# A Griffin block with two FFNs in split fp32r on one core: the second FFN begins in round 14 instead of round 10, two units a round

## The reference

```
t   = rmsnorm(x) * n1
xb  = causal_conv4(t @ Wx)
r,i = sigmoid(xb @ Wa), sigmoid(xb @ Wi)
a   = exp(-8 softplus(lam) r);  b = sqrt(max(1 - a*a, 1e-12)) * i * xb
h   = scan(h = a*h + b)
h1  = x + (h * gelu(t @ Wy)) @ Wo
u   = rmsnorm(h1) * n2
ffn = (gelu(u @ Wg) * (u @ Wu)) @ Wd          # first FFN, 256 -> 1024 -> 256
x1  = layernorm(x + h1 + ffn)
out = layernorm(x1 + relu(x1 @ W1 + b1) @ W2 + b2)   # second FFN
```

## Time and profile before

| | |
|---|---|
| median of 3 runs | 600.15 us (599.4 to 600.36) |
| the profiled execution | 600.54 us, its span 598.7 us |
| PE busy | 590.6 us (99% of the span), 3529 matmuls |
| DVE busy | 381.5 us (64%) |
| ACT busy | 317.2 us (53%) |
| POOL busy | 187.1 us (31%) |
| DMA | 15.68 MB, mean 26 GB/s |
| granted TensorE clock | 0.999 |

### The profile page before, as it was taken

The page is one execution under the profiler, slowest core; times in us unless marked ns, Lnnn a source line. Parts: engine busy times, 40 slices in busy tenths (PEclk is TensorE's granted clock), DMA queues, the critical chain, the costliest instruction groups (busy, mean ns, idle before and its releaser), DMA issues.

```text
span 598.7 us, 9284 instructions
## 1 busy us (share of the span) xinstructions
PE 590.6 (99%) x3529; PEld 521.7 (87%) x3529; DVE 381.5 (64%) x700; ACT 317.2 (53%) x601; POOL 187.1 (31%) x287
## 2 busy tenths in 40 slices
PE   8999999999999999999999999999999999999996
PEld 7768888899888998889898988889888898889896
DVE  5889877374856567484774846857478474662565
ACT  5988853654438444375443744356444653323454
POOL 3041353117240352313513153140722215240130
PEclk9999999999999999999999999999999999999999
DMA  8530010001001010010100001010000100010011
GB/s 283 166 106 1 1 36 1 2 1 36 1 1 35 2 37 0 1 36 2 35 2 19 18 1 36 1 36 2 1 1 0 37 2 0 2 36 0 1 37 36
DMA packets 13100, 15.68 MB, mean 26 GB/s; under 512 B 616, under 2 KB 12288, under 8 KB 13056
## 3 DMA queue, kind: packets, MB, share of 16 engines
q1 hardware_dynamic: 13056, 15.09, 7.5%
HBM read 10.89 MB, written 4.19 MB: 25 GB/s over the span
## 4 chain that ended last, share of the span: by engine, by line
PE 91%; DVE 5%; ACT 1%; issue 1%; DMA 1%; POOL 1%; SPq 0%; DVEq 0%
PE psum L361 17%; PE psum L363 17%; PE psum L362 17%; PE psum L372 11%; PE psum L374 11%; PE psum L373 11%; PE psum L379 3%; DMA xs<-in_L_attn_x_dram 1%; PE psum L447 1%; PE psum L575 1%; PE psum L577 1%; PE psum L573 1%; DVE row L1285 1%; PE psum L474 1%; PE psum L414 1%
## 5 line engine op out<-in xcount | busy, mean ns | idle before, releaser
L1662 POOL TENSOR_SCALAR gu_hi<-gu_raw 128x512 fp32r<-128x512 f32 x64 | 52.8, 824 | 313.1 <-DVE gu_raw L1308 310.3
L1318 DVE TENSOR_TENSOR hid_lo<-hid_raw,hid_hi 128x512 fp32r<-128x512 f32 x56 | 45.6, 814 | 84.0 <-ACT hid_hi L952 84.0
L948 ACT ACTIVATE hid_raw<-psum,vecs 128x512 f32<-128x512 f32 x56 | 38.5, 687 | 113.8 <-PE psum L363 113.8
L1308 DVE TENSOR_TENSOR gu_raw<-psum,gu_raw 128x512 f32<-128x512 f32 x64 | 44.1, 689 | 68.4 <-PE psum L363 68.1
L372 PE MATMUL psum<-w_d_hi,gu_hi 128*128 128x256 f32 x256 | 72.8, 284 | 0.2 <-DVE gu_lo L1313 0.2
L372 PE MATMUL psum<-w_hi,hid_hi 128*128 128x256 f32 x256 | 71.7, 280 | 0.2 <-DVE hid_lo L1318 0.2
L374 PE MATMUL psum<-w_hi,hid_lo 128*128 128x256 f32 x256 | 71.8, 281 | 0.0
L374 PE MATMUL psum<-w_d_hi,gu_lo 128*128 128x256 f32 x256 | 71.8, 281 | 0.0
L373 PE MATMUL psum<-w_lo,hid_hi 128*128 128x256 f32 x256 | 71.7, 280 | 0.0
L373 PE MATMUL psum<-w_d_lo,gu_hi 128*128 128x256 f32 x256 | 71.7, 280 | 0.0
L939 ACT ACTIVATE gu_raw<-psum 128x512 f32<-128x512 f32 x64 | 38.3, 598 | 48.6 <-PE psum L363 48.0
(11 more groups left out here) (222 smaller groups left out, 1519.3 us busy)
## 6 DMA issues: line engine op xcount, KB each, us to landing
out_dram<-row SPq DMA_DIRECT2D x15, 256.0 KB, 2.2
xs<-in_L_attn_x_dram SPq DMA_DIRECT2D x7, 512.0 KB, 3.5
raw<-in_L_ffn_W_dram SPq DMA_DIRECT2D x2, 1024.0 KB, 7.9
raw_gud<-in_L_attn_Wg_dram SPq DMA_DIRECT2D x1, 1024.0 KB, 7.4
raw_gud<-in_L_attn_Wu_dram SPq DMA_DIRECT2D x1, 1024.0 KB, 9.5
raw_gud<-in_L_attn_Wd_dram SPq DMA_DIRECT2D x1, 1024.0 KB, 12.7
xs<-in_L_attn_x_dram SPq DMA_DIRECT2D x2, 256.0 KB, 2.9
raw_xyai<-in_L_attn_Wx_dram SPq DMA_DIRECT2D x1, 256.0 KB, 2.6
```

The costliest lines, as they stand in the source:

```text
L948: nc.scalar.activation(hid_raw[:, w % SLOTS, :], bank[:, :], ACT.Relu, bias=vec("b1", m)).then_inc(relu_ready, 1)
L1308: nc.vector.tensor_tensor(gu_raw[:, r % SLOTS, :], up_bank(r)[:, :], gu_raw[:, r % SLOTS, :], ALU.mult).then_inc(gu_ready, 1)
L1318: nc.vector.tensor_tensor(hid_lo[:, w % SLOTS, :], hid_raw[:, w % SLOTS, :], hid_hi[:, w % SLOTS, :].bitcast(FP32), ALU.subtract).then_inc ...
L1662: nc.gpsimd.tensor_scalar(gu_hi[:, r % SLOTS, :], gu_raw[:, r % SLOTS, :], 1.0, 0.0, ALU.mult, ALU.add).then_inc(gu_hi_ready, 1)
```

## The change

**The second FFN.** It begins in round 14 (`FROM`). Rounds 14 to 17 have two units each, and from round 18 (`PACED`) it is again 10 units behind the first. Its splits and chunk 0's way to it move: W1's first piece is split in rounds 9 (hi) and 10 (lo), W1's second and W2's first in 10 and 11, W2's second in 13; chunk 0's statistics in round 11, its normalise in 12, `transpose_x1` at the end of 13, and the split of x1T at the start of 14. Chunk 2's `mix_out`, `add_mix`, `square_h1`, `norm_u` and `transpose_u` move one round on, into rounds 14 and 15.

**Banks.** Gate and up use banks 4 and 5 in rounds 9, 11 and 13 too. From round 18 on they alternate between 0 and 1, and `mlp_up(w)` uses bank w % 2. It waits for `gelu_gate` of its round.

**Rounds 0 to 7.** gate(1) stands ahead of up(0), down(r) moves from round r + 1 to r + 2, and mix_decay(1) with mix_input(1) from round 3 to round 4. Behind round 7 chunk 1's transposes alternate with mix_x(2).

**The prologue.** The first norm's root is taken by ScalarE (`Sqrt` with a table of its own, then `Exp`'s) and VectorE's reciprocal instead of GpSimd's power; the gates' first half alternates Wa and Wi by k; `second_x` is cut by k and put around `first_out`; steps of ScalarE and VectorE are reordered; x + h1 of chunk 0 goes from GpSimd to VectorE in round 3 (`first_add_x`), and SP's load of chunk 2 waits for it. W1 loads in two halves, and W2 behind chunk 2.

The core of the diff:

```diff
-LAG_DOWN = 11
+FROM = 14
+        PACED = KH + LAG_UP
+        ASIDE = (1, 3, 5, 9, 11, 13)
+        def second_units(r):
+            if r < FROM:
+                return ()
+            if r < PACED:
+                return (2 * (r - FROM), 2 * (r - FROM) + 1)
+            return (r - LAG_UP,)
         def gate_bank(r):
-            return psum[SECOND] if r in (1, 3, 5) else psum[GATE]
+            if r < PACED:
+                return psum[SECOND] if r in ASIDE else psum[GATE]
+            return psum[r % 2]
         def up_bank(r):
-            return psum[SECOND + 1] if r in (1, 3, 5) else psum[UP]
+            if r < PACED:
+                return psum[SECOND + 1] if r in ASIDE else psum[UP]
+            return psum[1 - r % 2]
+        def mlp_bank(w):
+            return psum[w % 2]
...
 # TensorE
             def mlp_up(w):
-                if r < UNITS:
-                    pe.wait_ge(gu_ready, r + 1)
+                if w < KH:
+                    pe.wait_ge(gu_ready if w % 2 else gelu_ready, FROM + w // 2 + 1)
+                elif r < UNITS:
+                    pe.wait_ge(gelu_ready, r + 1)
...
             def first_period(r):
-                gate_up(r)
-                if 1 <= r < KH - 1:
-                    down(r - 1)
-                if r == 3:
+                if r != 1:
+                    gate(r)
+                if r == 0:
+                    gate(1)
+                if r >= 2:
+                    down(r - 2)
+                if r == 4:
                     split_done("a", "i")
                     mix_decay(1)
                     mix_input(1)
+                up(r)
...
             def round_of(r):
-                if units(r - LAG_UP):
-                    mlp_up(r - LAG_UP)
-                if units(r - LAG_DOWN):
-                    mlp_down(r - LAG_DOWN)
+                if r == FROM:
+                    split_done("1", "2")
+                for w in second_units(r):
+                    mlp_up(w)
+                    if w == 1:
+                        mix_out(n)
+                    if w >= 1:
+                        mlp_down(w - 1)
+                    if w == 2:
+                        transpose_u(n)
-                if m == 1 and 1 <= p <= CHUNKS:
+                if r == KH + 5 or m == 1 and 2 <= p <= CHUNKS:
                     transpose_x1(p - 1)
...
 # ScalarE, at the end of round_of(r)
+                if r == KH + 1:
+                    weight_hi("1", ks=[0])
+                if r == KH + 2:
+                    weight_hi("1", ks=[1])
+                    weight_hi("2", ks=[0])
+                if r == KH + 5:
+                    weight_hi("2", ks=[1])
...
 # VectorE, in round_of(r)
-                if r == KH or m == 1 and f >= 1 and first:
+                if r == KH + 4 or m == 1 and f >= 1 and first:
                     normalise(f, 0, 0, x1_ready)
                     normalise(f, 0, 1, x1_ready)
-                if m == 2 and first:
+                if (r == FROM or m == 2 and f >= 1) and first:
                     split_lo(x1T_lo, x1T_hi, x1T_hi_ready, x1T_lo_ready, f)
...
                     if m == 5:
                         gated(n)
-                        hy_lo(n)
+                        if p >= 2:
+                            hy_lo(n)
...
                 if units(r):
                     gate_lo(r)
...
+                    if r == KH + 5:
+                        hy_lo(n)
...
+                for w in second_units(r):
+                    hidden_lo(w)
+                    if w == 2:
+                        split_lo(uT_lo, uT_hi, uT_hi_ready, uT_lo_ready, n)
+                if r == KH + 2:
+                    weight_lo("1", ks=[0])
+                if r == KH + 3:
+                    statistics(0, 0, 0, s1_ready)
+                    statistics(0, 0, 1, s1_ready)
+                    weight_lo("1", ks=[1])
+                    weight_lo("2", ks=[0])
+                if r == KH + 5:
                     weight_lo("2", ks=[1])
```

More of the change, by code:

```diff
@@ L77, in griffin_mlp_kernel @@
         h1.append(sb("h1_1", [P, TT, D]))
-        with nc.sbuf_tensor("raw_2", [P, WIDTH], FP32) as raw:
-            raw_of["2"] = raw[:, :]
-        rows = [sb(f"row{i}", [P, TT, D]) for i in range(2)]
+        rows = [sb("row0", [P, TT, D])]
+        with nc.sbuf_tensor("raw_1", [P, H], FP32) as raw:
+            raw_1 = [raw[:, :]]
+        rows.append(sb("row1", [P, TT, D]))
         normed = sb("normed", [P, TT, D])
@@ L381, in transposed, with transposed_by_pairs @@
                     last.then_inc(done, 1)
-            def transposed_by_pairs(src, c, ready, done, bank, fillers):
-                for q in range(PAIRS):
-                    pe.wait_ge(ready, 4 * c + 2 * q + 2)
+            def transposed_by_pairs(src, c, ready, done, bank, fillers, qs=range(PAIRS)):
+                for q in qs:
+                    if ready is u_ready:
+                        if c == 0:
+                            pe.wait_ge(first_u_ready, q + 2)
+                            if q == 1:
+                                pe.wait_ge(ready, u_tiles(0))
+                        else:
+                            pe.wait_ge(ready, u_tiles(c - 1) + 2 * q + 2)
+                    else:
+                        pe.wait_ge(ready, 4 * c + 2 * q + 2)
                     for tt in (2 * q, 2 * q + 1):
@@ L435, in first_x, with second_x @@
                         last.then_inc(half_wx_done if h == 0 else wx_done, 1)
[L437 to L442, removed]
+            def second_x(m, k):
+                pe.wait_ge(second_tT_ready[k], 1)
+                if k == 0:
+                    pe.wait_ge(tanh_i_ready, KD)
+                last = raw_step(psum[MIX + m][:, :], "x", m, k, first_tT[1])
+                if k == KD - 1:
+                    last.then_inc(wx_done, 1)
             def half_step(bank, n, k, h, moving):
@@ L742, in _ @@
                 first_y(h)
-            second_x(0)
+            for m in range(KD):
+                second_x(m, 0)
             pe.wait_ge(w_loaded["o"], DMA)
@@ L770, in square_first_x @@
                     last.then_inc(x_squared, 1)
+                    tiles = slice(2 * q, 2 * q + 2)
+                    act.wait_ge(rms_eps_ready, 1)
+                    act.wait_ge(x_squared, q + 1)
+                    nc.scalar.activation(rstd1[:, tiles], ss1[:, tiles], ACT.Sqrt, bias=rms_eps[:, :],
+                                         scale=1.0 / D).then_inc(rms1_ms, 1)
             def square_x(c):
@@ L1489, in lam_stepped @@
                 dve.wait_ge(lam_step, steps)
-            first_norm_t(0)
+            for q in range(PAIRS):
+                first_norm_t(q)
+            dve.wait_ge(vecs_ready, 1)
+            dve.wait_ge(tT_done, 1)
+            for f in range(KD):
+                nc.vector.tensor_scalar(first_tT[0][:, f, half(0)], pair_bank(MIX, 0)[:, f, :], vec("n1", f), None,
+                                        ALU.mult).then_inc(first_tT_ready[0], 1)
             dve.wait_ge(lam_exp, 1)
@@ L1676, in round_of @@
                     return
-                if r == KH:
-                    for q in range(PAIRS):
-                        ln_scale(0, 0, q)
                 if mixing:
```

242 lines of the change are left out of this document (138 added, 104 removed).

## The result

The changed kernel takes 602.14 us (median of 6 runs, 601.99 to 602.37), the kernel before 599.72 us in runs beside it (6 runs, 599.4 to 600.36). The ratio is 1.0040, with a 95% interval of 1.0028 to 1.0052: slower by 2.4 us. The forecast was 600.4 with a range of 598.3 to 602.0; the measured time lies 0.14 us above the range, and 2.4 us is more than the 1.2 us that the prediction could not tell from no change: it is the slower class, which had a chance of 0.18.

The account below looks back on a forecast made before the run. TensorE, busy for 99% of the span, was taken to bound the kernel, so the forecast counted its idle time. The terms -0.3 - 1.1 + 2.1 - 0.4 = +0.3 us on 600.15 gave 600.4, range 598.3 to 602.0.

Parts of the forecast that it names:

- the slower class: The outcome that the change makes the kernel slower, made up of rivals (c) and (d); chance 0.18.
- the sum of +0.3: Whole kernel: gains of 0.3, 1.1 and 0.4 us against a loss of 2.1, so 0.3 us slower.
- the part on rounds 14 to 17: Second FFN, two units a round: splits have 1.4 us or more each; hid_lo(4) costs 0.1 at most.
- round 60: From round 18 mlp_up waits for gelu instead of gate_times_up, which removes idle; gain 0.4 us.
- the prologue's step: Start to gate(8): gate(0) at 35.0 instead of 36.08, only 0.15 through to mix_decay(1), gate(8) gains 0.3 us.
- Rival (a): First rounds: TensorE's early lead gets through, gate(8) gains 1.3 us instead of 0.3, total 599.4; chance 0.15.
- Rounds 8 to 11: From gate(8) to gate(12): TensorE's idle falls from 1.37 to 0.25 us; gain 1.1.
- Rival (c): Rounds 8 to 13: VectorE becomes the bound and gu_lo comes late for down, total 602.2 us; chance 0.13.
- Round 14: New wait: mlp_up(0) needs a long chain's end, e + 16.8, against 14.7 us of TensorE work; loss 2.1.
- rival (b): Round 14's wait is absent or 0.3 us because sqrt and scan steps move closer together, total 598.6; chance 0.22.
- Round 15: Tightest later place: TensorE has 8.3 us of work before transpose_u(2), covering the norm by 2; no wait.
- rival (d): Round 15: chunk 2's norm is late by more than the 2 us of cover, total 601.9; chance 0.05.

Follow-up runs that it names:

- e1_conv: The changed kernel with VectorE's hid_lo(6) of round 17 moved ahead of the last tap of chunk 3's convolution; 600.90 us.
- e7_before: The kernel before, unedited, profiled a second time; that execution took 599.65 us.
- e8_act: The changed kernel with hid_lo(6) and W2's second split earlier, chunk 2's hy_lo later, and round 4's square roots ahead of gelu(4) on ScalarE; 601.97 us.
- e3_hy: The changed kernel with VectorE's hy_lo(2) moved from the end of round 13 to round 14, behind x1T_lo; 601.91 us.
- e6_banks: The kernel before with gate, up and mlp_up alternating between two banks from round 18 on, with the changed kernel's waits; 599.32 us.
- e5_start: The changed kernel with the second FFN back to one unit a round from round 10, W1 split in rounds 1 to 3, W2 in 8 and 9; 603.82 us.
- e9_act_old: e6_banks with ScalarE's square roots for the scan put ahead of gelu(4) in round 4, saving one table switch; 602.06 us.

## Why the prediction was wrong

The mechanism of round 14 was right, the sum of +0.3 was 2.04 us short of the table's +2.34, and one step accounts for most of that.

**The step that failed** is in the part on rounds 14 to 17: "relu, hid_lo and the other splits have 1.4 or more each" and, of hid_lo(4), "cost 0.1 at most". Nothing in the prediction says what stands ahead of hid_lo(6) on VectorE. In the trace TensorE is ready 1.3 us after relu(6) is done, near the 1.4 and enough for a hid_lo of 0.7 if VectorE were free. But in round 17 chunk 3's convolution is in front of it: four halves between gu_lo(17) and hid_lo(6), 2.7 us. In the kernel before the same four halves stand ahead of a hid_lo too (161.26 to 163.91 in the execution of the earlier trace rows), but TensorE wants that one a round later; with two units a round it is wanted in the same round. The start of mlp_down(6) is 0.99 us later than its spacing allows, and e1_conv shows the price: 1.24 us for undoing that alone. For hid_lo(4) in round 16, mlp_down(4) starts 0.27 late where 0.1 was allowed. The sum had nothing for either. With 0.2 for the slower blocks behind these two waits that is 1.46 of the 2.04. The rest is 0.33 in rounds 12 to 14, 0.15 in rounds 8 to 11 and 0.13 at gate(8), less 0.03 in round 60.

**The baseline.** The difference was added to 600.15, and the prediction read a profiled execution whose start was 0.8 late. The median of the kernel before with more runs is 599.72. So the forecast difference of +0.3 meant 600.0, and the measured difference is +2.4. The late start flattered the prologue's step too: gate(0) came to 34.62, earlier even than the forecast 35.0, but that is only 0.73 ahead of the more typical execution, e7_before. In the other profiles of kernels with the new prologue it is between 34.29 and 34.65.

**The prologue: right in the main.** Where 0.15 was to get through, mix_decay(1) is 0.01 earlier, with gate(4) ahead of it as worked out, and gate(8) 0.17 earlier where 0.3 was forecast. One of the two reasons given did not come as told: gu_lo(1) starts at 45.10, not 46.4, and down(0) and down(1) lose 0.2 together, not 0.3 to 0.5. That the forecast is still near is in part luck: the lead at the first down was smaller too, 1.53 against e7_before (0.17 at down(0), with one product more done) where 2.0 was forecast, and the two misses cancel. The waits behind come where they were put: 0.79 by the starts ahead of gate(7) (forecast 0.8), 0.55 at mix_out(1) (0.4). Rival (a), by which the lead gets through, is out. From the first step on mix_decay(1)'s result (53.17 in both kernels) to the last hy_hi (71.61, and 71.64 in e7_before) ScalarE's rows in the two kernels agree within 0.04 us, although TensorE has a whole product less to do in between. That fits ScalarE's queue as what holds the lead, but does not show it: e8_act, which shortened that queue, changed another wait with it.

**Rounds 8 to 11: right.** 0.95 of 1.1. The forecast had gate(12) start near 104.3 from a gate(8) at 83.4; it is 103.73 from 82.71. The gu_lo(8) that comes late for down(8) is there, with 0.16 by the starts and 0.11 in the block behind it. Rival (c), VectorE as the bound of these rounds, is out.

**Round 14: right in place, cause and size.** The chain was put at e + 16.8, from e, the end of gate(12). In the trace e is 105.09 and mlp_up(0) starts at 121.94: e + 16.85. ScalarE's part of it, which answers to the earlier trace rows:

```profile
107.20 1.52 ACT L956 ACTIVATE decay<-decay,half_c 128x512 f32<-128x512 f32 x2
108.63 1.14 ACT L963 ACTIVATE xv<-decay 128x512 f32<-128x512 f32 x2
...
111.08 1.16 ACT L968 ACTIVATE xv<-xv 128x512 f32<-128x512 f32 x2
```

and VectorE's, which answers to the earlier trace rows:

```profile
116.51 1.04 DVE L1351 TENSOR_TENSOR gy<-gy,xv 128x512 f32<-128x512 f32 x1
117.47 0.68 DVE L1420 TENSOR_TENSOR gu_lo<-gu_raw,gu_hi 128x512 fp32r<-128x512 f32 x1
118.07 1.28 DVE L1357 TENSOR_TENSOR mT_lo<-gy,mT_hi 128x512 fp32r<-128x512 f32 x2
119.28 1.21 DVE L1462 TENSOR_TENSOR w_lo<-raw_gud,w_hi 128x1024 fp32r<-128x1024 f32 x1
120.41 1.28 DVE L1228 TENSOR_TENSOR x1T_lo<-psum,x1T_hi 128x512 fp32r<-128x512 f32 x2
```

These stand one behind the other, as forecast, and rival (b), by which they move together, is out. By the starts TensorE loses 1.60 at mlp_up(0) and 0.55 at x1's transposes, 2.15 for a forecast of 2.1, and some 0.2 more in the blocks behind (last section). What the prediction did not see is that the chain has a second leg of the same length on ScalarE (e3_hy).

The squares start at 108.63 and the square roots at 111.08, 2.45 later: 1.14 of squares (until 109.77) and 1.31 for the one table switch between them. The Trainium skill ("ScalarE: Activation LUTs", What ACT_TABLE_LOAD costs) has 2.66 us for the switch, with a drain of 1.38 in it; the trace leaves no room for the drain, and the end of the chain, e + 16.85, agrees with the rows and not with the page.

**Round 15 and round 60: right.** There is no wait in round 15, so rival (d) is out, and round 60 gives back 0.43 (forecast 0.4).

The prediction's list of what would show it had "no wait from round 15 on", and the waits of rounds 16 and 17 came. Of the four rivals none named them. The slower class was given 0.18 for two other reasons.

## What to carry to other kernels

A step's cover has two ends: when its input is there, and when its own engine's queue reaches it. When work is moved so that a product is wanted in the same round instead of the next, walk every queue of that round in order and look at what stands ahead of each producer; an edit that moves one instruction ahead of two others was worth half of the loss here. Where a wait is at the end of a chain, look for a second leg of the same length before cutting a step, and cut the step that lies in both. And take the baseline from several executions: two profiles of the same kernel differed by 0.7 us at gate(0) and stayed apart by 0.8, and the one of e6_banks was 1.8 us late before any of its edit was reached.

## What the runs showed of the hardware that was not expected

**An idle stretch can cost more than itself.** In e5_start TensorE stands still for 3.33 us, and the granted clock falls behind it (windows of 4 us; busy time, granted clock, DMA share, GB/s):

```profile
94.00:98.00 4.00, 1.10 (x10) 1.00 0.00 0
98.00:102.00 4.00, 3.57 (x9) 0.57 0.00 0
102.00:106.00 4.00, 4.00 (x18) 1.00 0.00 0
```

A mean of 0.57 means that most of this window ran at the lower of the clock's two levels, 1.2 GHz instead of 2.4. mlp_up(0), the product behind the wait, takes 2.70 us for 1.37, and gate(11) behind it 1.65. The mean clock of the whole execution is 0.996 or 0.997 in all five executions of e5_start. The same is seen in e9_act_old behind a wait of only 1.78 us (the two windows, then the first matmul of down(4) and of the gate behind it):

```profile
64.00:68.00 4.00, 2.22 (x14) 0.87 0.00 0
68.00:72.00 4.00, 4.00 (x15) 0.71 0.00 0
```

```profile
65.88 0.36 PE L377 MATMUL psum<-w_d_hi,gu_hi 128*128 128x256 f32 x1 [1.78 <-DVE gu_lo L1323]
...
67.72 0.63 PE L366 MATMUL psum<-uT_hi,w_g_hi 128*128 128x512 f32 x1
```

There a gate product that takes 1.36 us elsewhere takes 2.56 (67.72 to 70.28), and the down ahead of it 1.84 for 1.41: 1.6 us on top of the 1.8 of waiting. Only this execution, 602.81 us, was profiled, but the mean granted clock is on record for all five of that kernel: 0.996 in those of 602.81 and 602.71 us, 0.999 or 1.000 in those of 601.64, 601.77 and 602.06. So the clock seems to have fallen in two of five executions of one kernel. In the changed kernel a wait of 1.44 us (ahead of 121.94) left the granted clock at 1.00, and in e8_act three waits of 0.97, 0.59 and 0.31 us within seven microseconds did so too. In these runs, then, a wait of 1 to 2 us sometimes took the clock with it and sometimes did not.

**The block behind a short wait is slower too.** With the clock at 1.00 the first matmuls of mlp_up(0) start 0.31 apart and the next ones 0.23, where packed ones have 0.2275 throughout; the block takes about 0.1 us more. In the changed kernel's rounds 12 to 17 four blocks start late by 0.55, 1.60, 0.27 and 0.99, 3.41 in all, and the loss there is 3.89. No wait in the list shows the other 0.48. Some 0.4 of it is in the blocks right behind the four waits (mlp_up(0) takes 1.46 for 1.365, mlp_down(4) and mlp_down(6) 1.53 for 1.41), and 0.1 is in gate(14), which takes 1.48 behind x1's transposes; in the kernel before the same transposes have a slower gate behind them too (1.46, at 90.94 in e7_before), only ahead of gate(12). A block behind transposes shows the same 0.31 at its start without any idle (136.78 to 137.09), so a wait is not the only thing that makes a block start slowly.
